# Second attention of a hybrid layer: other layout and transfers for the stacked bf16 rows, another way of adding the residual

## The reference

```python
Q, K, V = proj(wq, bq), proj(wk, bk), proj(wv, bv)        # 16 heads of 8
scores = jnp.einsum('bhqd,bhkd->bhqk', Q, K) * scale
u = min(L, max(1, int(np.log(L))))                         # 6
top_u = jax.lax.top_k(scores.max(axis=-1), u)[1]           # 6 queries of each head
q_sel = jnp.take_along_axis(Q, top_u[..., None], axis=2)
attn = jax.nn.softmax(jnp.einsum('bhud,bhkd->bhuk', q_sel, K) * scale, axis=-1)
ctx = jnp.einsum('bhuk,bhkd->bhud', attn, V)
padded = jnp.zeros((B, H, L, d_k)).at[bi, hi, top_u].set(ctx)
out = padded.transpose(0, 2, 1, 3).reshape(B, L, D) @ wo.T + bo
x = x + out
```

## Time and profile before

| | |
|---|---|
| time, median of 3 runs | 1387.65 us (1384.28 to 1389.28) |
| the profiled execution | 1385.65 us |
| its span, first to last instruction | 1383.8 us |
| granted TensorE clock, mean | 0.871 of full speed |
| busy in the span: PE, DVE, ACT, POOL | 81%, 75%, 55%, 64% |
| second attention, first to last score | 525.2 to 1115.1 us |

### The profile page before, as it was taken

How to read it: one execution, slowest core, us unless ns; L and a number is a source line. 1 busy time by engine, 2 the same in 40 slices (tenths; PEclk the granted TensorE clock), 3 DMA queues, 4 the chain that set the end, 5 groups by cost and what they waited for, 6 DMA issues and landing times.

```text
span 1383.8 us, 27422 instructions
## 1 busy us (share of the span) xinstructions
PE 1121.0 (81%) x7574; PEld 696.9 (50%) x7574; DVE 1040.6 (75%) x4507; ACT 754.2 (55%) x1934; POOL 885.4 (64%) x1342
## 2 busy tenths in 40 slices
PE   3999999897999987888878888888888899999100
PEld 1555555564888972334333333334333379899100
DVE  2899999898475636899989999998988966565211
ACT  2444444342665655777766766766766657556000
POOL 3237776677553503567888888878785555367776
PEclk9999999999899995798898888977868789999655
DMA  6877621102465664444444444444444435577522
GB/s 177 220 192 192 164 70 60 51 31 57 121 187 176 191 174 120 118 112 102 114 105 107 107 112 114 115 120 114 105 105 97 132 89 162 160 217 213 150 76 78
DMA packets 176104, 176.65 MB, mean 128 GB/s; under 512 B 22736, under 2 KB 166224, under 8 KB 175952
## 3 DMA queue, kind: packets, MB, share of 16 engines
q1 hardware_dynamic: 159568, 141.19, 38.4%
q0 software_dynamic: 16384, 33.72, 8.8%
HBM read 83.91 MB, written 90.92 MB: 126 GB/s over the span
## 4 chain that ended last, share of the span: by engine, by line
PE 22%; DVE 21%; POOL 10%; ACT 6%; issue 5%; DMA 3%; SPq 2%; ACTq 0%; POOLq 0%; DVEq 0%
DVE pT L1544 13%; PE pair L2028 5%; PE pair L1951 5%; POOL tok L663 5%; POOL vmyg L663 5%; ACT pT L1059 3%; PE pair L1962 2%; PE pair L1940 1%; PE bank L2069 1%; PE bank L1752 1%; PE bank L2013 1%; DVE xs L1466 1%; SPq L461 1%; PE bank L1758 1%; PE bank L2034 1%
## 5 line engine op out<-in xcount | busy, mean ns | idle before, releaser
L1544 DVE CUSTOM_DVE_ANT_0 pT<-pair,pT 128x256 f32<-128x256 f32 x1024 | 379.6, 414 | 46.8 <-ACT pT L1059 44.3
L1059 ACT ACTIVATE pT<-pair 128x256 f32<-128x256 f32 x1024 | 322.9, 398 | 137.7 <-PE pair L2028 136.9
L1951 PE MATMUL pair<-xeT_sg,unit_w 128*128 128x256 f32 x768 | 183.4, 382 | 0.0
L1269 DVE TENSOR_TENSOR pT<-pair,causal 128x512 f32<-128x512 f32 x256 | 159.4, 679 | 15.5 <-PE pair L1813 15.2
L604 POOL DMA_INDIRECT dispA<-xnf,sli x128 | 128.4, 1003 | 53.9 <-issue 31.6
L2028 PE MATMUL pair<-whose,apart 64*128 64x512 bf16 x512 | 135.3, 454 | 33.7 <-DVE smax L1544 29.7
L604 POOL DMA_INDIRECT dispB<-xnf,sli x128 | 128.5, 1004 | 51.9 <-issue 30.7
L2028 PE MATMUL pair<-xeT_sg,apart 64*128 64x512 bf16 x512 | 132.9, 451 | 31.6 <-DVE smax L1544 30.8
L1436 DVE TENSOR_TENSOR hid<-xeT_sg,pair 128x512 f32<-128x512 f32 x96 | 65.9, 686 | 114.6 <-ACT xeT_sg L969 114.4
L1951 PEld LDWEIGHTS pair<-xeT_sg,unit_w 128*128 128x128 f32 x768 | 139.6, 192 | 15.2
L1962 PE MATMUL pair<-unit_w,hid 128*128 128x128 f32 x768 | 103.7, 279 | 12.1 <-DVE ye L1450 12.1
(11 more groups left out here) (257 smaller groups left out, 2382.9 us busy)
## 6 DMA issues: line engine op xcount, KB each, us to landing
dispB<-zeros SPq DMA_DIRECT2D x16, 1419.0 KB
apart<-dispA SPq DMA_DIRECT2D x96, 129.0 KB
apart<-dispB SPq DMA_DIRECT2D x96, 129.0 KB
ybufA<-ye SPq DMA_DIRECT2D x48, 256.0 KB
ybufB<-ye SPq DMA_DIRECT2D x48, 256.0 KB
apart<-q_rows SPq DMA_DIRECT2D x128, 96.0 KB
q_rows<-ctxT SPq DMA_DIRECT2D x64, 128.0 KB, 2.5
whose<-k_rows SPq DMA_DIRECT2D x64, 96.0 KB
```

The lines of the kernel that those rows point to most:

```text
L1059: act.activation(rel[n % RING][:, q, :], pair[n % RING][:, q, HALF:SEQ], ACT.Relu).then_inc(s["relu_done"], 1)
L1269: dve.tensor_tensor(pT[n % (2 * NG)][:, :, :], bank[4 + n % 4].rearrange("p (j t) -> p j t", j=GH), causal[:, :].unsqueeze(1).to_broadcast ...
L1544: dve.tensor_tensor_reduce(out=rel[n % RING][:, q, :], in0=pair[n % RING][:, q, 0:HALF], in1=rel[n % RING][:, q, :], scale=1.0, scalar=LOW ...
L1951: last = pe.matmul(bank[3 + 2 * h + k][:, u * UR:(u + 1) * UR], unit_w[r][:, u, k * D:(k + 1) * D], xeT[h][:, UT * u:UT * (u + 1), :].rear ...
```

## The change

The projections' columns (`b_wqT`, `b_wkT` and their biases) are permuted before the kernel, from (head pair, even or odd, feature) to (even or odd, feature, head pair). `q_rows` and `k_rows` become slot, partition, token. So one slot, one feature and one of even or odd is a run of 8 rows, 8 KB, and a whole partition of a stack is one run. A stack is read in six transfers without halves; parts that are needed twice are written by one transfer with the source repeated: 18 transfers a batch instead of 32. TensorE waits for both whole stacks before pair 0. A second mask of heads (`headposb`, `headofb`) fits the permuted order; it takes a memset and a select on GpSimd and a reduction on VectorE at the start.

The residual: `scatter_context` first multiplies the identity with `xs` of the batch into `bank[1]`, and the four matmuls are added to it. ScalarE copies the bank to `xs`, after its pair 0 of the next batch, and VectorE waits for the copy before its next use, at pair 9.

ScalarE loads the registers of a group's expert numbers one group earlier. The first batch's stacks are issued at groups 18, 19, 20 and 21 as queries out, keys out, queries in, keys in.

```diff
-Q_SLOTS = ((0, 3), (1, 4), (2,))
-K_SLOTS = ((0,), (1,), (2,))
+Q_SLOTS = (slice(0, 5, 3), slice(1, 5, 3), slice(2, 3))
+K_SLOTS = (slice(0, 1), slice(1, 2), slice(2, 3))
...
-Q_OUT = 16 * 5
-K_OUT = 16 * 3
-ROWS_IN = 16 * 2 * 2 * len(Q_GROUPS)
+ROWS_OUT = 16 * 3
+ROWS_IN = 16 * 2 * len(Q_GROUPS)
...
-        q_rows = [nc.dram_tensor(f"q_rows{h}", [H, 5, DH, SEQ], BF16).ap() for h in range(2)]
-        k_rows = [nc.dram_tensor(f"k_rows{h}", [H, 3, DH, SEQ], BF16).ap() for h in range(2)]
+        q_rows = [nc.dram_tensor(f"q_rows{h}", [5, P, SEQ], BF16).ap() for h in range(2)]
+        k_rows = [nc.dram_tensor(f"k_rows{h}", [3, P, SEQ], BF16).ap() for h in range(2)]
...
-            def rows_out(n, rows, parts, slots, ready, done):
+            def rows_out(n, kind, rows, parts, slots):
...
-                        sp.dma_start(rows[n % 2][:, slot], part).then_inc(s[done], 16)
-            def rows_in(n, rows, stack, groups, half):
-                t = slice(half * STACKS // 2, (half + 1) * STACKS // 2)
-                each = rows[n % 2].rearrange("(t g) s d n -> g (s d) t n", g=2)
+                for part, at, nth in zip(parts, slots, ("first", "second", "third")):
+                    sp.wait_ge(s[f"{kind}_{nth}"], n + 1)
+                    to = rows[n % 2][at].rearrange("s p n -> p s n")
+                    sp.dma_start(to, part.unsqueeze(1).to_broadcast(list(to.shape))).then_inc(s[f"{kind}_rows_done"], 16)
+
+            def rows_in(n, kind, rows, stack, groups):
+
+                sp.wait_ge(s[f"{kind}_rows_done"], ROWS_OUT * (n + 1))
                 for g in range(2):
                     at = g * NP * DH
                     for first, count in groups:
-                        sp.dma_start(stack[n % 2][at:at + count * DH, t, :], each[g][first * DH:(first + count) * DH, t, :]).then_inc(
-                            s[f"rows_in{2 * (n % 2) + half}"], 16)
+                        sp.dma_start(stack[n % 2][at:at + count * DH, :, :].rearrange("p t n -> p (t n)"),
+                                     rows[n % 2][first:first + count, g * P // 2:(g + 1) * P // 2, :].rearrange(
+                                         "s (d t) n -> s d (t n)", t=STACKS)).then_inc(s[f"{kind}_in{n % 2}"], 16)
                         at += count * DH
...
             def first_stack(g):
                 if g == 18:
                     queries_out(0)
+                if g == 19:
+                    keys_out(0)
                 if g == 20:
                     queries_in(0)
-                    keys_out(0)
-                if g == 22:
+                if g == 21:
                     keys_in(0)
...
                     if 2 <= g < G - 2:
-                        copies(g + 2, weights_of(mybir.EngineType.Activation, seg, g + 2, 1))
+                        copies(g + 2, ex)
+                    if 1 <= g < G - 3:
+                        ex = weights_of(mybir.EngineType.Activation, seg, g + 3, 1)
...
+            def residual(b):
+                act.wait_ge(s["bo_done"], b + 1)
+                act.activation(xs[:, tiles_of(b), :].rearrange("p t d -> p (t d)"), bank[1][:, :], ACT.Copy).then_inc(s["x1_ready"], 1)
...
             def residual(b):
-                dve.wait_ge(s["bias_added"], b + B + 1)
-                dve.wait_ge(s["bo_done"], b + 1)
-                xb = xs[:, tiles_of(b), :]
-                dve.tensor_tensor(xb, xb, bank[1][:, :].rearrange("p (t d) -> p t d", t=TB), ALU.add).then_inc(s["x1_ready"], 1)
                 dve.wait_ge(s["x1_ready"], b + B + 1)
...
-                if n % (PAIRS // 2) == 0:
-                    pe.wait_ge(s[f"rows_in{2 * h + n // (PAIRS // 2)}"], ROWS_IN * (b // 2 + 1))
+                if n == 0:
+                    pe.wait_ge(s[f"q_in{h}"], ROWS_IN * (b // 2 + 1))
+                    pe.wait_ge(s[f"k_in{h}"], ROWS_IN * (b // 2 + 1))
...
+                pe.wait_ge(s["bias_added"], b + B + 1)
+                pe.matmul(bank[1][:, :], ident[:, :], xs[:, tiles_of(b), :].rearrange("p t d -> p (t d)"), start=True, stop=False)
                 for t in range(TB):
-                    last = pe.matmul(bank[1][:, t * D:(t + 1) * D], sel[:, t * P:(t + 1) * P], cwo[:, :], start=True, stop=True)
+                    last = pe.matmul(bank[1][:, t * D:(t + 1) * D], sel[:, t * P:(t + 1) * P], cwo[:, :], start=False, stop=(t == TB - 1))
```

More of the change, by code:

```diff
@@ L124, in build @@
         headof = sb("headof", [P, H])
+        headposb = sb("headposb", [P, H // 2, 2, DH])
+        headofb = sb("headofb", [P, H])
         inturn = sb("inturn", [P, GH])
@@ L441, in begin @@
                     load(seg, r)
-            def rows_out(n, rows, parts, slots, ready, done):
+            def rows_out(n, kind, rows, parts, slots):
                 if n >= 2:
[L447 to L451, removed]
-                        sp.dma_start(rows[n % 2][:, slot], part).then_inc(s[done], 16)
-            def rows_in(n, rows, stack, groups, half):
-                t = slice(half * STACKS // 2, (half + 1) * STACKS // 2)
-                each = rows[n % 2].rearrange("(t g) s d n -> g (s d) t n", g=2)
+                    sp.wait_ge(s[f"{kind}_in{n % 2}"], ROWS_IN * (n // 2))
+                for part, at, nth in zip(parts, slots, ("first", "second", "third")):
[4 more added lines that the diff above has]
+                sp.wait_ge(s[f"{kind}_rows_done"], ROWS_OUT * (n + 1))
                 for g in range(2):
@@ L460, in rows_in @@
                     for first, count in groups:
-                        sp.dma_start(stack[n % 2][at:at + count * DH, t, :], each[g][first * DH:(first + count) * DH, t, :]).then_inc(
-                            s[f"rows_in{2 * (n % 2) + half}"], 16)
+                        sp.dma_start(stack[n % 2][at:at + count * DH, :, :].rearrange("p t n -> p (t n)"),
+                                     rows[n % 2][first:first + count, g * P // 2:(g + 1) * P // 2, :].rearrange(
+                                         "s (d t) n -> s d (t n)", t=STACKS)).then_inc(s[f"{kind}_in{n % 2}"], 16)
                         at += count * DH
             def queries_out(n):
-                rows_out(n, q_rows, q_part, Q_SLOTS, ("q_first", "q_second", "q_third"), "q_rows_done")
+                rows_out(n, "q", q_rows, q_part, Q_SLOTS)
             def keys_out(n):
-                rows_out(n, k_rows, k_part, K_SLOTS, ("k_first", "k_second", "k_third"), "k_rows_done")
+                rows_out(n, "k", k_rows, k_part, K_SLOTS)
             def queries_in(n):
-                sp.wait_ge(s["q_rows_done"], Q_OUT * (n + 1))
                 if n >= 2:
                     sp.wait_ge(s["bsc_done"], 2 * PAIRS * (n - 1))
-                for half in range(2):
-                    rows_in(n, q_rows, qst, Q_GROUPS, half)
+                rows_in(n, "q", q_rows, qst, Q_GROUPS)
             def keys_in(n):
-                sp.wait_ge(s["k_rows_done"], K_OUT * (n + 1))
-                for half in range(2):
-                    rows_in(n, k_rows, kst, K_GROUPS, half)
+                rows_in(n, "k", k_rows, kst, K_GROUPS)
             def first_stack(g):
@@ L551, in _ @@
             pool.memset(headpos[:, :, :], 0.0)
+            pool.memset(headposb[:, :, :, :], 0.0)
             pool.memset(ohsum[:, :], 0.0)
@@ L569, in _ @@
                                pattern=[[-DH, H], [-1, DH]], channel_multiplier=1)
+            pool.affine_select(out=headposb[:, :, :, :], in_=headposb[:, :, :, :], compare_op=ALU.not_equal, fill=1.0, base=0,
+                               pattern=[[-1, H // 2], [-DH * (H // 2), 2], [-(H // 2), DH]], channel_multiplier=1)
             bv = block8[:, :].rearrange("p (h d) -> p h d", d=DH)
@@ L1017, in keys_first @@
                 if n:
-                    act.wait_ge(s["k_rows_done"], K_OUT * n)
+                    act.wait_ge(s["k_rows_done"], ROWS_OUT * n)
                 act.activation(k_part[0], kTb[n % 3][:, 0:SEQ], ACT.Copy).then_inc(s["k_first"], 1)
@@ L1063, in body @@
                     first_half_above(b, n)
+                    if before and n == 0:
+                        residual(b - 2)
                     if last and n == 5:
@@ L1111, in pieces @@
             def pieces(g):
+                if g == 0:
+                    residual(B - 2)
                 if g == 1:
@@ L1124, in pieces @@
                     context_x(B - 1)
+                if g == 10:
+                    residual(B - 1)
                 if g == 13:
@@ L1139, in _ @@
             dve.wait_ge(s["consts2"], 1)
+            dve.tensor_reduce(headofb[:, :], headposb[:, :, :, :].rearrange("p t g d -> p (t g) d"), AX.X, ALU.add)
             dve.tensor_reduce(headof[:, :], headpos[:, :, :], AX.X, ALU.add).then_inc(s["headof_done"], 1)
@@ L1611, in body @@
                     largest(b, h, n)
-                    if before and n == 0:
-                        residual(b - 2)
                     if b == MID + 2 and n == 29:
@@ L2248 @@
         arrays[n] = np.ascontiguousarray(np.asarray(inputs[src]).T)
```

(3 more changed lines are left out.)

10 lines of the change are left out of this document (5 added, 5 removed).

## The result

| | before | after |
|---|---|---|
| median | 1387.33 us (4 runs) | 1729.96 us (4 runs, 1728.86 to 1731.89) |
| span of the profiled execution | 1383.8 us | 1726.8 us |
| first score of the second attention | 525.2 us | 544.9 us |
| first to last score | 589.9 us | 912.2 us |

The account below looks back on a forecast made before the run. VectorE was taken to set the pace mid-batch, with almost no slack in the stacks' DMA path at the seams. 24.5 us a batch in 15 batches, 368, plus 23 at the start: 1385.65 + 391 = 1777 us, range 1640 to 1960.

Parts of the forecast that it names:

- How many engines: Stack transfers: the DRAM side's outermost count of 3 or 2 leaves three or two DMA engines each; chance 0.82.
- The price of a stack: Stack reads: the busiest engine carries 393 KB at 22 GB/s, so a stack takes 17.9 us.
- The chain of a batch: Second attention: query stack, key parts, key stack, then scores add to 61.4 us a batch against 36.9.
- the range's lower end: Batch at 22.7 GB/s with early request and key parts not held up: 54.1 us, 1659 in all, set at 1640.
- The start: Before the first score: first stacks and the expert stores behind them delay it from 525.2 to near 548, 23 us.
- The six issues: SyncE: issuing a stack's six transfers takes at most 2.5 us, where twelve took 4.87.
- The residual: Identity matmul (1.13 to 2.00 us), ScalarE's copy (0.60) and VectorE's saved 0.68 fall into the wait, counting nothing.
- Loads, masks, order at the start: Start and expert stage: mask work and earlier register loads cost nothing, the loads 2 us at most.
- The rivals: Spread stack transfers: VectorE gains, 1374 us (0.07), or TensorE late at the seam, 1405 (0.06); one engine, over 2600 (0.02).
- The second rival: Seam between batches: spread transfers, but identity matmul and copy delay TensorE 1.0 to 1.9 us a batch, 1405 us; chance 0.06.

Follow-up runs that it names:

- the kernel of sixteen rows: The changed kernel with one transfer a slot for even and odd heads together, 16 rows to partitions 8 apart: 1379.16 us, ratio to before 0.9949.
- the merged layout: The changed kernel with DRAM rows ordered even or odd, slot, row, so slots merge; each part written by two transfers: 1422.44 us, ratio to before 1.0295.
- the merged, alternating kernel: The merged layout with a stack's transfers alternating between even and odd heads instead of all even first: 1408.64 us, ratio to before 1.0158.

## Why the prediction was right

**How many engines.** Right, and it was the step that mattered: 16 small packets a stack and a DMA share of 0.137, as foretold (16, about 0.15); given 12 and 16 engines back, 308 of 343 us vanish, with sixteen all of them. That the transfers of a stack share the same three, which the prediction held for likely, shows too: all six of the query stack are asked for within 4.25 us, and still hardly ever more than three packets are under way. The rule of the Trainium skill that stands in the prediction agrees with every count taken here: 3 and 2, 8, 12 and 16 small packets a transfer.

**The price of a stack.** 22 GB/s an engine was assumed, 21.3 measured. The query stack of batch 8 lay 17.9 us between first and last packet (17.9 assumed), the key stack 19.1. There was luck in it: the rate of one quiet store was taken over for three engines, and the prediction has no term for a rate that falls with their number; eight engines with the same runs came to 10.4.

**The chain of a batch.** Its form was right: query stack, then key parts behind it, then key stack, then scores, and both stacks add. The period was 58.7 us in the mean ((1426.1 - 544.9) / 15 from first scores) instead of 61.4, which is 40 us in 15 batches. In the mean of these batches the query stack is asked for after 18.8 us (20 foretold), its last packet lands 18.8 later (0.9 + 17.9), the keys are asked for 1.5 behind that (2.8), their last packet lands 19.1 later (18.8), and the first score follows after 0.5 (1.0). So the stacks were right and three smaller terms too large. Every one of the 15 batches begins 0.53 to 0.55 us behind its key stack's last packet: that is what TensorE's long waits wait for. The sum for the range's lower end has the 0.9 us of a first packet once where the chain has it twice; with both it is 1672 instead of 1659, which changes nothing here.

**The start.** First score foretold near 548, measured 544.9: 19.7 us of loss for 23. The cause is the one named: the stacks of batch 0 have landed at 540.1 (542.5 foretold), and what the first score waits for are the last expert results, which VectorE holds back for the stores behind the stacks:

```profile
525.79 0.69 DVE L1463 TENSOR_TENSOR ye<-pair,wrow 128x512 f32<-128x512 f32 x1 [14.73 <-DMA ybufB<-ye]
544.93 1.04 PE L2037 MATMUL pair<-whose,apart 64*128 64x512 bf16 x4 [0.79 <-DVE ye L1463]
```

**The six issues.** Wrong, without effect: "at most 2.5 us", taken from a price per transfer of another form, were 4.25. The engines were busy for much longer.

**The residual.** Identity matmul, copy and VectorE's 0.68 us were to fall into the wait and count nothing. For the matmul this holds in the changed kernel: pair 0 waits 21.7 us behind it. It doesn't hold for the copy, which ScalarE makes behind pair 0's two operations, when the wait is over:

```profile
1071.01 0.66 ACT L1065 ACTIVATE pT<-pair 128x256 f32<-128x256 f32 x2 [23.87 <-PE pair L2037]
1071.56 0.60 ACT L1054 ACTIVATE xs<-bank 128x512 f32<-128x512 f32 x1
```

No loss shows from it: the query stack is asked for 18.8 us after the first score in the mean, in the kernel before 19.9. Put into the kernel before, the three together make no difference to the time.

**Loads, masks, order at the start.** Counted as 0 to 2 us. They weren't tried alone. The stretch behind the last score grew by 1.0 us, and the kernel of sixteen rows, which has them all, starts its first score at 522.5, before the 525.2 of the earlier trace rows.

**The rivals.** Their condition, spread transfers, was made in the merged layout, and neither 1374 nor 1405 came out but 1422; with sixteen rows a transfer it was 1379. The rivals took a spread stack to land earlier than today; 8 KB runs on 12 neighbouring rows take 7.8 us instead of 7.3, and the halves are worth 7 us. The second rival's place, TensorE at the seam, is what ends last there once the stacks are quick, in the kernel of sixteen rows.

**What stays open.** Why eight or more engines on neighbouring 8 KB runs fall to 10 to 12 GB/s each, while three run at 21; and why the merged, alternating kernel loses another 17 us to the one before (1408.6 - 1385.0, less the 7 of the halves). Where they lie the profiled executions show: a batch takes 38.6 us in the mean, against 37.6 in the kernel before without halves, and 0.9 of this lies between the request for the query stack and that for the key stack (10.4 and 9.5 us), where the key parts go out. They do so in six transfers instead of three and behind packets of 8 KB instead of 1 KB; which of the two costs it was not separated.

## What to carry to other kernels

Before making runs longer, write down the outermost dimension of both sides of the transfer as they are after merging: a slot that is sliced out of the middle of a part did not merge with the next here, and the count of slots, 3 or 2, not that of partitions, was the number of engines. Count the small packets of one transfer in the trace: in every transfer counted here they were the engines. And where a stage is a chain of transfers that wait for one another, a slower transfer counts in full as often as it stands in the chain, while work on engines that wait there anyway counts nothing.

## What the runs showed of the hardware

- Engines don't add up with 8 KB runs. Per busy engine: 21.3 GB/s on three, 10.4 on eight with neighbouring partitions, 12.5 on twelve to sixteen with neighbouring rows, 18.5 on eight with partitions 4 apart and a slower pace of issue, 1.05 / (0.535 x 16 x 7) = 17.5 on sixteen with partitions 8 apart. 1 KB runs on twelve had 13.5.
- The price of an issue on SyncE differs with the form of the transfer: 0.34 us with 8 neighbouring partitions (5.41/16), 0.65 with 8 that lie 4 apart (10.32/16), 0.61 with 16 that lie 8 apart (4.91/8), 0.71 with unmerged slots (4.25/6), 0.39 with merged slots (2.32/6), 0.41 in the kernel before.
